# A decoder layer on one core: new hand-written orders for the first stage, the loop and the stores

## The reference

```python
x = _layernorm(x + _L0_attn_ref(x, w_q, w_k, w_v, w_o, gate, M, z))            # linear attention over batch pairs
x = _layernorm(x + _L0_xattn_ref(ctx, ctx, x, ssm_kernel, D, 8))               # Hyena-like long convolution
x = _layernorm(x + _L0_ffn_ref(x, gate_up_packed, gate_up_scales, down_packed, down_scales))   # fp4 gated FFN

# xattn: outer products of k and v in heads of 8, causal convolution with ssm_kernel along the
# 512 features (rfft/irfft of length 1024), plus kv * D, contracted with q
kv = jnp.einsum('bhil,bhjl->bijhl', k_, v_)
y = jnp.fft.irfft(jnp.fft.rfft(kv, n=1024) * jnp.fft.rfft(ssm_kernel, n=1024), n=1024)[..., :L]
out = jnp.einsum('bijhl,bhil->bjhl', y + kv * D[None, None, None, :, None], q_)
# ffn
h = jax.nn.silu(gate) * up
y = jnp.einsum('bsi,hi->bsh', h, w_down)
return y / rms
```

## Time and profile before

| | us |
|---|---|
| median of three runs | 551.12 (550.42 to 551.61) |
| the profiled execution | 551.09 |
| its span | 549.4 |
| PE busy | 519.1 (94%) |
| ACT, POOL, DVE busy | 414.9, 388.8, 387.6 |
| mean granted clock of TensorE | 0.990 |
| start of c0 (convolution of group 0) | 86.19 |
| g0_0 of iteration 1 | 128.98 |
| y1_0, the first step of iterations 2, 3, 4, 7 | 177.50, 233.80, 286.16, 443.23 |
| last transpose of iteration 7, first gate piece of iteration 8 | 493.85, 495.99 |

### The profile page before, as it was taken

How to read it: one execution, slowest core, us unless ns; L and a number is a source line. 1 busy time by engine, 2 the same in 40 slices (tenths; PEclk the granted TensorE clock), 3 DMA queues, 4 the chain that set the end, 5 groups by cost and what they waited for, 6 DMA issues and landing times.

```text
span 549.4 us, 11955 instructions
## 1 busy us (share of the span) xinstructions
PE 519.1 (94%) x3798; PEld 395.0 (72%) x3798; DVE 387.6 (71%) x1153; ACT 414.9 (76%) x978; POOL 388.8 (71%) x449
## 2 busy tenths in 40 slices
PE   6799999999999899999999999999999999998991
PEld 5678888788776577677767776777677767755660
DVE  2877789998769567876787777777776877763223
ACT  3456774357998788788878987898689868868981
POOL 2686885974996399859976996799679849861231
PEclk9999999999999899999999999999999999999997
DMA  8700454223100630113012210311031101001001
GB/s 215 202 0 29 150 162 129 76 58 117 39 2 9 217 122 2 59 59 114 2 58 95 77 46 12 115 57 57 0 117 36 38 19 59 2 2 39 1 20 38
DMA packets 26594, 36.44 MB, mean 66 GB/s; under 512 B 4474, under 2 KB 13818, under 8 KB 26554
## 3 DMA queue, kind: packets, MB, share of 16 engines
q1 hardware_dynamic: 26554, 35.94, 21.4%
...
## 4 chain that ended last, share of the span: by engine, by line
PE 83%; DVE 5%; POOL 4%; ACT 3%; issue 3%; DMA 1%; POOLq 0%; SPq 0%; DVEq 0%
PE p_cv L142 7%; PE p_cv L144 7%; PE p_cv L143 7%; PE p_n L1282 6%; PE p_n L1283 6%; PE p_n L1284 6%; PE p_qk L1269 5%; PE p_qk L1271 5%; PE p_x L1269 5%; PE p_x L1271 5%; PE p_ct L100 4%; PE p_s L1271 4%; PE p_s L1269 4%; PE p_qk L891 3%; PE p_n L902 2%
## 5 line engine op out<-in xcount | busy, mean ns | idle before, releaser
L1123 ACT ACTIVATE p_qk<-p_qk,rescale 128x256 f32<-128x256 f32 x192 | 78.4, 451 | 26.1 <-PE p_qk L1271 25.7
L142 PE MATMUL p_cv<-kv_hi,toe 128*128 128x288 f16 x320 | 91.6, 286 | 0.1
L144 PE MATMUL p_cv<-kv_hi,toe 128*128 128x288 f16 x320 | 91.6, 286 | 0.0
L143 PE MATMUL p_cv<-kv_lo,toe 128*128 128x288 f16 x320 | 91.6, 286 | 0.0
L1091 POOL TENSOR_TENSOR h_lo<-w,h_hi 128x256 f16<-128x256 f32 x88 | 59.3, 681 | 38.9 <-ACT h_hi L1140 38.3
L301 POOL TENSOR_TENSOR shared<-shared 128x1024 f32<-128x1024 f32 x32 | 75.5, 2359 | 14.9 <-DVE shared L261 14.8
L1123 ACT ACTIVATE p_x<-p_x,rescale 128x256 f32<-128x256 f32 x192 | 78.8, 457 | 5.4 <-PE p_x L1271 4.7
L1269 PE MATMUL p_qk<-x_hi,wg_hi 128*128 128x256 f16 x256 | 63.3, 274 | 7.0 <-DVE x_lo L289 3.6
L227 DVE TENSOR_TENSOR kv_lo<-kv,kv_hi 128x1152 f16<-128x1152 f32 x32 | 60.4, 1887 | 11.4 <-ACT kv_hi L191 10.7
L1282 PE MATMUL p_n<-wd_hi,h_hi 128*128 128x512 f16 x176 | 67.3, 383 | 0.7 <-POOL h_lo L1091 0.7
L1283 PE MATMUL p_n<-wd_lo,h_hi 128*128 128x512 f16 x176 | 67.2, 382 | 0.0
...
## 6 DMA issues: line engine op xcount, KB each, us to landing
toe<-toeplitz_rows SPq DMA_DIRECT2D x16, 512.0 KB, 3.8
...
ring<-in_x SPq DMA_DIRECT2D x6, 512.0 KB, 3.7
x_rows<-ring SPq DMA_DIRECT2D x6, 512.0 KB, 3.4
...
```

Of the source, the lines that this page charges most:

```text
L142: nc.tensor.matmul(dst, hi, kh, start=(mb == 0), stop=False)
L143: nc.tensor.matmul(dst, hi, kl, start=False, stop=False)
L144: done = nc.tensor.matmul(dst, lo, kh, start=False, stop=(mb == lb))
L1123: done = nc.scalar.activation(sums, sums, ACT.Copy, scale=rescale[:, p - 1, part * GI + i:part * GI + i + 1])
```

## The change

No instruction is added or removed. START_SYNC, the four START lists, the four loop lists and the beginning of LAST_PE hold the same steps in another order, and SyncE issues its last two stores the other way round. In the start, x of slot 0 is turned before w_q, and of the steps of iteration 1 the down products come last; xt1 stands before b0 on DVE. In the loop, d0 and d1 come last on PE, behind xt1 and y0_10. The diff, cut:

```diff
@@ -1074,8 +1074,8 @@
         body(NG - 2, ctx=False)
         body(NG - 1, nxt=False)
         store(NG - 2, 1)
+        store(NG - 1, 1)
         store(NG - 1, 0)
-        store(NG - 1, 1)
         for t in range(GT):
             sp.wait_ge(stored[t], 16 * NG)
 
@@ -1322,54 +1322,54 @@
-    START_SYNC = ("cx2 x3 x4 st0 x5 cx3 tw0 toe1 st1 toe0 x6 st2 st3 xq0 xq1 xr1 x7 xr0 xq3 toe2 cx4 xq2 xq5 st4 xr3 "
-                  "cx5 xr2 toe3 xq4 toe4 st5 cx6 st6 toe5 st7 cx7").split()
+    START_SYNC = ("cx3 x3 x4 cx2 st0 tw0 x5 toe1 toe0 st1 cx4 st2 x6 st3 x7 xq0 xq1 xq3 xq2 toe2 xr0 xr1 xq5 cx5 xq4 "
+                  "xr3 toe3 st4 toe4 xr2 st5 cx6 st6 cx7 toe5 st7").split()
-    START_PE = ("iw0 Xa0 iw1 Xb0 iw2 iw3 iz0 Q0 V0 S0 M0 Xa1 N0 Xb1 f0 w0 w1 w2 Q1 Xa2 T0 w3 f1 Oa0 w4 Ob0 w5 w6 V1 "
...
-                "w28 Q5 T4 w29 w30 Oa4 Ob4 w31 w32 Xa6 V5 q0 c0 c1 q1 Xb6 c2 c3 M5 c4 f2 c5 S5 f3 c6 N5 Xa7 c7 c8 Q6 "
-                "c9 T5 c10 c11 Oa5 rt0 c12 Ob5 c13 c14 V6 c15 S6 q2 M6 Xb7 N6 q3 Q7 rt1 T6 +c0 +c1 Oa6 xt0 Ob6 S7 xt1 "
-                "V7 +g0_0 +g1_0 M7 N7 +g0_1 +g1_1 +c2 +g0_2 +g1_2 +c3 +c4 T7 +g0_3 +g1_3 +ct0 +g2_0 +c5 Oa7 +g3_0 "
...
-                "+g8_1 +g7_3 +ct1 +y0_1 +g8_2 +y0_2 +g9_0 +y0_3 +qt0 +g10_0 +g9_1 +y0_4 +y0_5 +g10_1 +rt1 +g9_2 +d0 "
-                "+g8_3 +g10_2 +g9_3 +y0_6 +qt1 +g10_3 +d1 +y0_7 +xt0 +y0_8 +y0_9 +y0_10 +xt1").split()
+    START_PE = ("Xa0 iw0 Xb0 iw1 iw2 iz0 Q0 iw3 V0 S0 Xa1 M0 N0 Xb1 f0 w0 w1 Q1 Xa2 T0 w2 f1 w3 Oa0 w4 w5 Ob0 S1 w6 "
+                "V1 w7 w8 Xb2 M1 N1 w9 Xa3 w10 Q2 T1 w11 w12 Oa1 Ob1 w13 w14 V2 w15 S2 M2 Xb3 N2 w16 w17 Q3 T2 w18 "
+                "w19 Oa2 Ob2 Xa4 w20 w21 V3 S3 w22 M3 Xb4 w23 N3 w24 Q4 T3 w25 w26 Oa3 Ob3 Xa5 w27 w28 V4 S4 M4 Xb5 "
+                "w29 N4 Q5 T4 w30 w31 Oa4 Ob4 w32 Xa6 V5 c0 c1 q0 Xb6 M5 q1 S5 c2 c3 c4 N5 c5 c6 c7 Q6 c8 c9 T5 f2 "
+                "c10 Oa5 c11 f3 c12 Ob5 Xa7 rt0 c13 V6 c14 c15 q2 S6 q3 Xb7 M6 N6 Q7 rt1 +c0 T6 +c1 Oa6 xt0 Ob6 S7 "
+                "xt1 V7 +g0_0 +ct0 M7 N7 +g1_0 +g0_1 +c2 +g1_1 +g0_2 +c3 +g0_3 T7 +g1_2 +c4 +g2_0 +c5 +g1_3 +g2_1 "
+                "+g3_0 +c6 +g2_2 Oa7 +g4_0 +g2_3 +g3_1 +g4_1 +c7 +g3_2 +g5_0 +c8 +g4_2 +g3_3 +c9 +g5_1 +g4_3 +c10 "
+                "+g5_2 +g6_0 +c11 +g6_1 +g5_3 +g7_0 +g6_2 +rt0 +c12 +c13 +g7_1 +g8_0 +g6_3 +ct1 +g7_2 +c14 +g8_1 +c15 "
+                "+g7_3 +g9_0 Ob7 +g8_2 +g10_0 +g9_1 +y0_0 +y0_1 +g10_1 +y0_2 +qt0 +g9_2 +g10_2 +g8_3 +rt1 +g9_3 +y0_3 "
+                "+y0_4 +qt1 +g10_3 +y0_5 +y0_6 +y0_7 +xt0 +y0_8 +y0_9 +y0_10 +xt1 +d0 +d1").split()
-    START_DVE = ("is0 fs0 sg0 u0 mk0 ig0 dn0 u1 o0 u2 ra0 rb0 sg1 bn0 mk1 dn1 o1 u3 ra1 rb1 sg2 bn1 mk2 nb0 dn2 o2 u4 "
...
-                 "tm8 kl3 tm9 sg6 tm10 tm11 ra5 tm12 rb5 tm13 tm14 bq0 tm15 mk6 nq0 bn5 dn6 kl4 o6 bq1 sg7 ra6 nq1 xl0 "
...
-                 "+gu8 +nm0 +gu9 nb5 +gu10 nb6 +nm1 +xt0 bn7 +a0 nb7 +b0 +xt1 +e0").split()
+    START_DVE = ("is0 fs0 sg0 u0 mk0 ig0 dn0 u1 o0 u2 sg1 ra0 rb0 bn0 mk1 sk0 dn1 nb0 o1 u3 ra1 rb1 sg2 bn1 mk2 dn2 o2 "
...
+                 "tm8 tm9 kl3 tm10 ra5 tm11 sg6 rb5 tm12 tm13 bq0 tm14 tm15 mk6 bn5 nq0 dn6 kl4 o6 bq1 sg7 ra6 nq1 xl0 "
...
+                 "+tm9 +gu3 nb6 +tm10 +lk3 +gu4 +tm11 +gu5 +bs0 +tm12 +tm13 ra7 +gu6 +tm14 +tm15 +gu7 rb7 +ln +bn0 bn7 "
+                 "+bs1 +nm0 +gu8 +bn1 +gu9 +gu10 nb7 +nm1 +xt0 +a0 +xt1 +b0 +e0").split()
-    START_ACT = ("kw0 xa0 kw1 xb0 ks0 kw2 kw3 re0 vk0 ge0 xa1 rv0 xb1 wh0 lc0 wh1 rv1 kt0 re1 ok0 wh2 wh3 wh4 wh5 wh6 "
...
-                 "+rs9_1 +kq0 +rs10_1 +rs9_2 +hh7 +rs10_2 +rs9_3 +gu8 +rs10_3 +gu9 +hh8 +kq1 +gu10 +hh9 +hh10 +xt0 nm5 "
-                 "+n0 nm6 +xt1 nm7").split()
+    START_ACT = ("xa0 kw0 xb0 kw1 kw2 ks0 re0 kw3 vk0 ge0 xa1 rv0 xb1 kt0 lc0 wh0 wh1 rv1 hk0 re1 wh2 ok0 wh3 wh4 wh5 "
...
+                 "+rs6_2 +hh4 +gu5 +rs7_1 +rs6_3 +hh5 +rs7_2 +rs8_1 +ct1 +gu6 +kn +rs7_3 +rs8_2 +gu7 +hh6 +rs9_1 +hh7 "
+                 "+rs10_1 +rs8_3 +rs9_2 +rs10_2 +kq0 +rs9_3 +rs10_3 +gu8 nm6 +hh8 +gu9 +gu10 +kq1 +hh9 +hh10 +xt0 nm7 "
+                 "+n0 +xt1").split()
-    START_POOL = ("id0 ms0 ws0 ws1 ws2 ws3 ws4 pr0 ws5 ws6 ws7 ws8 ws9 ws10 pw0 ws11 ws12 ws13 ws14 ws15 ws16 ws17 ws18 "
-                  "ws19 ws20 pw1 ws21 ws22 ws23 pw2 ws24 ws25 ws26 pr1 ws27 ws28 pw3 ws29 ws30 ws31 ws32 pr2 pw4 tr0 "
...
+    START_POOL = ("id0 ms0 ws0 ws1 pr0 ws2 ws3 ws4 ws5 ws6 ws7 ws8 ws9 ws10 pw0 ws11 ws12 ws13 ws14 ws15 ws16 ws17 ws18 "
+                  "ws19 ws20 ws21 pw1 ws22 ws23 ws24 ws25 ws26 pw2 ws27 ws28 pr1 ws29 pw3 ws30 ws31 ws32 pw4 pr2 tr0 "
...
-    PE_ORDER = ("y1_0 y1_1 y1_2 y1_3 g0_0 g1_0 g2_0 y1_4 g0_1 y1_5 g1_1 y1_6 g0_2 ct0 g1_2 g2_1 g0_3 c2 c3 g1_3 g3_0 "
-                "y1_7 g2_2 y1_8 c4 g4_0 g3_1 c5 g2_3 c6 g3_2 c7 g4_1 g5_0 y0_0 g3_3 g4_2 g5_1 c8 ct1 g4_3 c9 g5_2 "
-                "g6_0 c10 y1_9 c11 g5_3 g7_0 y1_10 g6_1 qt0 c12 g8_0 g7_1 y0_1 c13 g8_1 y0_2 rt0 g6_2 g7_2 g8_2 c14 "
-                "g6_3 c15 g7_3 g9_0 y0_3 y0_4 g9_1 g10_0 g9_2 qt1 g10_1 g8_3 y0_5 g9_3 g10_2 d0 rt1 y0_6 d1 g10_3 xt0 "
-                "y0_7 y0_8 y0_9 y0_10 xt1").split()
+    PE_ORDER = ("y1_0 g0_0 g1_0 y1_1 g0_1 g2_0 g1_1 y1_2 g0_2 y1_3 g1_2 g0_3 c2 g2_1 c3 g3_0 y1_4 g1_3 g2_2 g3_1 y1_5 "
+                "c4 g2_3 g4_0 c5 g3_2 g4_1 c6 c7 g5_0 g3_3 y1_6 g4_2 y1_7 g5_1 g6_0 ct0 c8 g4_3 y1_8 g6_1 c9 g7_0 c10 "
+                "g5_2 g7_1 c11 y1_9 rt0 g5_3 g6_2 g7_2 ct1 c12 y1_10 g6_3 qt0 g7_3 c13 g8_0 c14 g9_0 c15 g8_1 g10_0 "
+                "y0_0 g9_1 g8_2 g10_1 y0_1 g9_2 qt1 y0_2 g8_3 g10_2 y0_3 rt1 g9_3 y0_4 g10_3 xt0 y0_5 y0_6 y0_7 y0_8 "
+                "y0_9 xt1 y0_10 d0 d1").split()
-    DVE_ORDER = ("tm0 tm1 lk1 gu0 tm2 gu1 tm3 tm4 tm5 gu2 lk2 tm6 tm7 gu3 tm8 tm9 tm10 gu4 lk3 gu5 tm11 tm12 tm13 a1 "
-                 "bs0 bn0 tm14 gu6 tm15 gu7 ln b1 nm0 gu8 bs1 gu9 bn1 gu10 xt0 nm1 a0 xt1 b0 e0 e1").split()
+    DVE_ORDER = ("tm0 tm1 gu0 lk1 tm2 tm3 gu1 tm4 tm5 gu2 lk2 gu3 tm6 tm7 tm8 gu4 tm9 lk3 tm10 tm11 bs0 gu5 bn0 tm12 "
+                 "gu6 a1 tm13 tm14 gu7 tm15 b1 nm0 gu8 bs1 bn1 gu9 xt0 gu10 nm1 ln xt1 a0 e1 b0 e0").split()
-    ACT_ORDER = ("rv0 tl rs0_1 rs1_1 rs2_1 rs0_2 rs1_2 rs0_3 hk1 gu0 ct0 rs1_3 rs2_2 hh0 gu1 rs3_1 hh1 rs2_3 rs3_2 hk2 "
-                 "gu2 rs4_1 rs3_3 rv1 rs4_2 rs5_1 gu3 rs4_3 hh2 rs5_2 hh3 ct1 rs5_3 rs6_1 gu4 hk3 hh4 gu5 ho0 rs7_1 n1 "
-                 "rs6_2 rs8_1 kq0 rs7_2 rs8_2 rs6_3 rs7_3 hh5 rs8_3 gu6 kn gu7 rs9_1 hh6 hh7 rs9_2 rs10_1 rs9_3 rs10_2 "
-                 "gu8 kq1 ho1 gu9 rs10_3 hh8 hh9 gu10 xt0 hh10 n0 xt1").split()
+    ACT_ORDER = ("tl rs0_1 rs1_1 rs0_2 rs1_2 rs0_3 rs2_1 gu0 hk1 rs2_2 hh0 rs1_3 rs3_1 gu1 rs2_3 rv0 rs3_2 rs4_1 gu2 "
+                 "ho0 hk2 rs3_3 hh1 rs4_2 gu3 rs5_1 rs4_3 hh2 hh3 rs6_1 gu4 rs5_2 hk3 rs7_1 rs6_2 hh4 rs5_3 ct0 rs7_2 "
+                 "rv1 gu5 rs6_3 ct1 rs7_3 gu6 n1 kq0 hh5 rs8_1 hh6 gu7 rs9_1 hh7 rs8_2 rs10_1 rs9_2 rs8_3 rs10_2 kq1 "
+                 "rs9_3 gu8 ho1 rs10_3 gu9 hh8 gu10 xt0 hh9 kn hh10 xt1 n0").split()
-    POOL_ORDER = ("pr1 pr2 hl0 hl1 tr0 pr3 hl2 hl3 tr1 pn hl4 tr2 a1 hl5 bn0 tr3 hl6 hl7 hl8 hl9 bn1 hl10 a0 b1 b0").split()
+    POOL_ORDER = ("pr1 hl0 pr2 tr0 hl1 pr3 hl2 tr1 hl3 hl4 tr2 a1 hl5 bn0 hl6 hl7 tr3 pn hl8 bn1 hl9 hl10 b1 a0 b0").split()
-    LAST_PE = ("g0_0 g1_0 g2_0 y1_0 y1_1 g0_1 y1_2 g1_1 y1_3 y1_4 g0_2 g2_1 g1_2 y1_5 g0_3 g2_2 g1_3 y1_6 g3_0 g2_3 "
+    LAST_PE = ("y1_0 y1_1 y1_2 g0_0 g1_0 g2_0 g0_1 g1_1 y1_3 y1_4 g0_2 g2_1 g1_2 y1_5 g0_3 g2_2 g1_3 y1_6 g3_0 g2_3 "
```

More of the change, by code:

```diff
@@ L1344, in decoder_layer @@
-    START_ACT = ("kw0 xa0 kw1 xb0 ks0 kw2 kw3 re0 vk0 ge0 xa1 rv0 xb1 wh0 lc0 wh1 rv1 kt0 re1 ok0 wh2 wh3 wh4 wh5 wh6 "
[8 rows of a table removed]
-                 "+n0 nm6 +xt1 nm7").split()
-    START_POOL = ("id0 ms0 ws0 ws1 ws2 ws3 ws4 pr0 ws5 ws6 ws7 ws8 ws9 ws10 pw0 ws11 ws12 ws13 ws14 ws15 ws16 ws17 ws18 "
-                  "ws19 ws20 pw1 ws21 ws22 ws23 pw2 ws24 ws25 ws26 pr1 ws27 ws28 pw3 ws29 ws30 ws31 ws32 pr2 pw4 tr0 "
-                  "pr3 tr1 pr4 tr2 pq0 tr3 +pr1 pq1 pw5 +pr2 +tr0 +hl0 +pr3 +hl1 +tr1 +hl2 +hl3 +pn +tr2 +hl4 +hl5 +tr3 "
-                  "+hl6 +hl7 pw6 +bn0 +hl8 +bn1 +hl9 +hl10 pw7 +a0 +b0").split()
@@ new lines, in decoder_layer @@
+    START_DVE = ("is0 fs0 sg0 u0 mk0 ig0 dn0 u1 o0 u2 sg1 ra0 rb0 bn0 mk1 sk0 dn1 nb0 o1 u3 ra1 rb1 sg2 bn1 mk2 dn2 o2 "
[5 rows of a table added]
+                 "+bs1 +nm0 +gu8 +bn1 +gu9 +gu10 nb7 +nm1 +xt0 +a0 +xt1 +b0 +e0").split()
+    START_ACT = ("xa0 kw0 xb0 kw1 kw2 ks0 re0 kw3 vk0 ge0 xa1 rv0 xb1 kt0 lc0 wh0 wh1 rv1 hk0 re1 wh2 ok0 wh3 wh4 wh5 "
[8 rows of a table added]
+                 "+n0 +xt1").split()
+    START_POOL = ("id0 ms0 ws0 ws1 pr0 ws2 ws3 ws4 ws5 ws6 ws7 ws8 ws9 ws10 pw0 ws11 ws12 ws13 ws14 ws15 ws16 ws17 ws18 "
+                  "ws19 ws20 ws21 pw1 ws22 ws23 ws24 ws25 ws26 pw2 ws27 ws28 pr1 ws29 pw3 ws30 ws31 ws32 pw4 pr2 tr0 "
+                  "pr3 tr1 pr4 tr2 pq0 tr3 +pr1 pq1 pw5 +pr2 +hl0 +tr0 +hl1 pw6 +pr3 +hl2 +tr1 +hl3 +hl4 +pn +hl5 +tr2 "
```

(1 more changed line is left out.)

## The result

The changed kernel takes 543.59 us (median of four runs, 543.10 to 545.92), against 550.77 for the kernel before on the same chip: ratio 0.9876, 95% interval 0.9844 to 0.9908. The forecast was 543.7. The profiled execution is the longest of the four, 545.92 us, with a span of 544.2; the other three took 543.1 to 543.9.

| us | before | after | difference | forecast |
|---|---|---|---|---|
| start, to g0_0 of iteration 1 | 128.98 | 130.58 | +1.60 | -0.5 |
| iteration 1, g0_0 to y1_0 of iteration 2 | 48.52 | 49.71 | +1.2 | +0.4 |
| iteration 2 | 56.30 | 52.19 | -4.1 | -3.9 |
| iterations 3 to 6 | 209.43 | 209.33 | -0.1 | -0.8 |
| iterations 7 and 8, to the last matmul | 95.06 | 92.36 | -2.7 | -2.0 |

The account below looks back on a forecast made before the run. TensorE was taken as the bound, so only its stalls could go. The terms -3.9 - 0.8 - 1.5 - 0.5 - 0.6 - 0.5 + 0.4 = -7.4 turned 551.1 into 543.7 us; range 539.5 to 548.5, chance 0.8.

Parts of the forecast that it names:

- Iteration 2: With xt1 ahead of b0, TensorE's stall at the iteration's start and the clock drop behind it go: -3.9 us.
- The clock's share: In iteration 2, the time lost to the lower granted clock after the stall, taken as 1.4 us of the 4.65.
- Iterations 3 to 6: The loop's stall at g9_2 goes, with small waits at rt1, d0 and the first rescalings: -0.2 us each, -0.8 together.
- rival (a): The loop's stall only changes its name: rt1 and ln cost what g9_2 did or up to 0.4 more; 545.5 to 548.5, chance 0.22.
- it no longer meets tr3, but hl9 and hl10: In the loop, VectorE's ln now runs beside GpSimd's hl9 and hl10, 0.7 us each; by the skill's rule ln takes 0.6 longer.
- Iteration 7: The stalls at g9_2 and y0_10 go, rt1's 0.3 comes in, 0.8 of 2.3 us is left: -1.5.
- Iteration 8: The 1.7 us stall between xt1 and g0_0 goes, but g0_1 waits 0.8 and g1_1 0.3 for rescalings: -0.5.
- Stores: SyncE's last two stores swapped: the first goes out earlier and hides, the last issue ends 0.62 us earlier: -0.6.
- Start: The stretch up to g0_0 of iteration 1 keeps 0.5 us of a 1.4 us lead: -0.5, bounds -0.5 and 2.5.
- Q2 starts 1.4 us ahead: In the start reckoning, TensorE's step Q2 begins 1.4 us earlier than in the kernel before.
- V0's wait: In the start, V0 waits for all four copies and starts about 1 us later than in the kernel before.
- Iteration 1: One stall of 0.7 us goes, but g4_1 and g6_2 are short of cover and qt1 waits for bs1: +0.4, bounds -0.7 and 1.5.

Follow-up runs that it names:

- the eighth kernel: The changed kernel with gu4 of iteration 1 ahead of tm10 on DVE and ho0 of iteration 8 behind rs2_1 on ACT: 542.63 us, ratio 0.9848.

## Why the prediction was right, step by step

- **Iteration 2**, -3.9: -4.1, -3.94 by the START lists alone. The cause was read rightly (b0 ahead of xt1, then the clock), but not completely. The clock's share was put too low: 4.65 less 2.25 and 0.63 is 1.77, not 1.4, of which the trace has some 1.6 in matmuls at the lower level. The load behind nm5 and st5 was a second wait of 1.6 us which the prediction didn't see, since a trace shows only the latest of several. It mentioned nm6 ahead of xt1 and left SyncE's queue uncosted there. With the old ACT and SyncE orders the term would have been -1.8.
- **Iterations 3 to 6**, -0.2 each: -0.03. g9_2's stall went. The steps named in its place were wrong, rt1 and d0 don't wait; rival (a), that the stall changes its name, came true, though at y0_10 and not at the steps it named. The step that failed is "it no longer meets tr3, but hl9 and hl10": the contention was foreseen and put on ln (0.6 longer), when it falls on whichever starts second, hl10, by 0.95.
- **Iteration 7**, -1.5: -2.25. I let 0.8 of small stalls stay, and none did: y0_10 had no ln beside hl10 there.
- **Iteration 8**, -0.5: -0.44, with g0_1's stall 0.96 (0.8 foreseen) and g1_1's 0.28 (0.3).
- **Stores**, -0.6: -1.0. The issue was right at 0.64; what lies behind it gained some 0.4 more.
- **Start**, -0.5: -0.58. The size was right, the way there wasn't. The step that failed is "Q2 starts 1.4 us ahead": with the START lists alone Q1 is 2.6 ahead, but Q2 starts 1.29 later, and 0.4 of that remain when the work put ahead of it (Xa3 and w10, 0.88) is taken off. At c0 0.07 are left, with q0 (0.44) still to be done. The stalls between V0 and c0 only changed their names: S0, N0, w1, w2, Oa0, w5 and w6 before, V0, T0, w2, w3, w4, w5 and w10 now, 5.3 us in all then and 5.4 now. What is gained comes behind c0, at two steps of the kernel before that don't wait in the new order; the prediction had their 1.5 in brackets (N5 and T6, the two lines below this list). V0's wait was foreseen at its price and cost nothing.
- **Iteration 1**, +0.4: +1.2, near the bound of 1.5. Not g6_2 or qt1, but 1.22 at g7_0, for gu4 behind nb6, tm10 and lk3, and 0.42 at g4_0; g4_1's 0.20 was foreseen. Mis-sized since I checked covers on PE and not GpSimd, which is full there: the eighth kernel shows that the time stays when the stall goes.

```profile
95.87 0.60 PE L935 MATMUL p_n<-vext,AT 128*128 128x129 f32 x3 [0.55 <-DVE AT L750]
122.20 0.44 PE L857 MATMUL p_s<-ident,o 128*128 128x128 f32 x2 [0.65 <-DVE o L771]
```

That the total was right to 0.1 us was luck in good part: +0.8 (iteration 1) and +0.7 (iterations 3 to 6) against -0.75 (iteration 7), -0.4 (stores) and -0.2 (iteration 2), and the start's term right by another way than forecast.
